# Three probability buffers, a wait moved behind the transposes, an earlier copy of the values, and the last head's blocks shared

## The reference

```
x = x + tanh(g0) * experts(layernorm(x))        # 4 experts, one per token by its id: (silu(h Wg) * (h Wu)) Wd
x = x + tanh(g1) * block(layernorm(x))

def block(r):                                   # 16 heads of 32, F = 2048, R = 16
    a = rmsnorm(r, ln1_w)
    scores = (a Wq.T)(a Wk.T).T / sqrt(32), causal; probs = softmax(scores)
    attn = (probs (a Wv.T)) Wo.T
    mod = 0.1 * tanh(attn @ A)
    h = rmsnorm(r, ln2_w)
    gate = silu(h W_in.T + mod * (h @ A) @ B)
    return r + (gate * (h W_up.T)) W_down.T
```

## Time and profile before

| | |
|---|---|
| median of three runs | 1045.88 us |
| profiled execution, its own time | 1046.06 us |
| its span, first to last instruction | 1044.3 us |
| PE, PEld busy | 1011.3 (97%), 831.4 (80%) us |
| DVE, ACT, POOL busy | 701.9 (67%), 608.0 (58%), 284.6 (27%) us |
| mean granted TensorE clock | 0.996 |
| attention phases | about 172 to 247, 392 to 468, 613 to 688, 833 to 909 us |

### The profile page before, as it was taken

How to read it: one execution, slowest core, us unless ns; L and a number is a source line. 1 busy time by engine, 2 the same in 40 slices (tenths; PEclk the granted TensorE clock), 3 DMA queues, 4 the chain that set the end, 5 groups by cost and what they waited for, 6 DMA issues and landing times.

```text
span 1044.3 us, 16780 instructions
## 1 busy us (share of the span) xinstructions
PE 1011.3 (97%) x5140; PEld 831.4 (80%) x5141; DVE 701.9 (67%) x1837; ACT 608.0 (58%) x1447; POOL 284.6 (27%) x280
## 2 busy tenths in 40 slices
PE   6999999999999999999999999999999989999998
PEld 6787888777888887778888888778888877788887
DVE  7766755996665558985665479966655599854443
ACT  4464456997344448985444369963444489844432
POOL 4536124861000117650000148610001177400000
PEclk9999999999999999999999999999999999999999
DMA  6545133343222426443322354432334253322221
GB/s 236 195 151 171 40 121 96 77 119 132 94 90 90 131 62 169 97 133 115 104 91 91 111 157 92 117 122 91 92 102 147 64 149 92 91 81 90 90 90 51
DMA packets 47073, 115.78 MB, mean 111 GB/s; under 512 B 6800, under 2 KB 6800, under 8 KB 46096
## 3 DMA queue, kind: packets, MB, share of 16 engines
q1 hardware_dynamic: 43968, 105.06, 33.7%
q0 software_dynamic: 3040, 9.96, 2.8%
HBM read 76.46 MB, written 13.37 MB: 86 GB/s over the span
## 4 chain that ended last, share of the span: by engine, by line
PE 86%; DVE 11%; issue 1%; DMA 1%; POOL 1%; ACT 1%; SPq 0%; DVEq 0%; POOLq 0%
PE bank L534 68%; PE bank L731 7%; DVE big L1399 5%; PE bank L793 4%; DVE wr L1385 3%; PE bank L697 2%; PE bank L835 1%; PE bank L590 1%; PE bank L764 1%; PE bank L605 1%; PE bank L648 1%; DMA stack<-wr 0%; PE bank L570 0%; POOL wr L502 0%; DVE big L1422 0%
## 5 line engine op out<-in xcount | busy, mean ns | idle before, releaser
L534 PE MATMUL bank<-hT,wr 128*128 128x512 f32 x1488 | 358.2, 390 | 0.0
L534 PEld LDWEIGHTS bank<-hT,wr 128*128 128x128 f32 x1488 | 279.2, 188 | 60.8 <-issue 1.5
L534 PE MATMUL bank<-wr,actr 128*128 128x512 f32 (+1 forms) x1224 | 303.4, 397 | 2.2 <-DVE actr L1367 1.5
L534 PEld LDWEIGHTS bank<-wr,actr 128*128 128x128 f32 x1224 | 228.9, 190 | 50.8 <-issue 3.0
L490 POOL TENSOR_SCALAR big<-big,rr 128x256 f32<-128x256 f32 (+1 forms) x128 | 154.5, 1215 | 82.4 <-DVE rr L1405 82.4
L429 POOL TENSOR_TENSOR wqs<-wstage,wqs 128x512 fp32r<-128x512 f32 x32 | 43.1, 1358 | 433.6 <-ACT wqs L949 432.2
L1432 DVE SCALAR_TENSOR_TENSOR wr<-stream,lns,wr 128x256 fp32r<-128x256 f32 x256 | 121.7, 537 | 52.2 <-ACT wr L1059 52.2
L1033 ACT ACTIVATE big<-big,nb 128x512 f32<-128x512 f32 (+3 forms) x256 | 140.9, 557 | 11.5 <-DVE nb L1399 11.1
L1385 DVE TENSOR_TENSOR wr<-bank,wr 128x512 fp32r<-128x512 f32 (+1 forms) x224 | 126.0, 607 | 21.3 <-ACT wr L949 20.7
L949 ACT ACTIVATE wr<-bank 128x512 fp32r<-128x512 f32 (+1 forms) x224 | 110.1, 529 | 35.7 <-PE bank L534 20.2
L949 ACT ACTIVATE actr<-act_sb 128x512 fp32r<-128x512 f32 x64 | 40.4, 632 | 146.0 <-DVE act_sb L1446 146.0
(11 more groups left out here) (174 smaller groups left out, 988.0 us busy)
## 6 DMA issues: line engine op xcount, KB each, us to landing
stream<-in_wmlp SPq DMA_DIRECT2D x64, 512.0 KB, 4.0
stack<-wr SPq DMA_DIRECT2D x192, 128.0 KB, 2.3
stream<-in_wmlp SPq DMA_DIRECT2D x64, 256.0 KB, 2.7
big<-in_x SPq DMA_DIRECT2D x4, 1024.0 KB
big<-y_rows SPq DMA_DIRECT2D x4, 1024.0 KB, 5.8
residual<-big SPq DMA_DIRECT2D x4, 1024.0 KB
big<-residual SPq DMA_DIRECT2D x4, 1024.0 KB, 6.5
out<-big SPq DMA_DIRECT2D x3, 1024.0 KB, 4.8
```

The source lines that it names most:

```text
L534: mm = pe.matmul(dst, lhs(pl, k), rhs(pr, k), start=start and i == 0, stop=stop and i == n - 1, skip_group_check=skip)
```

## The change

Five edits.

1. Three probability buffers instead of two, taken by head modulo 3; the third lies at column 2048 of `big`, in `hb`. The maxima of head n wait for the transposes of head n-3, and those of heads 0 to 2 for none. The load of y now also waits for all transposes of its batch.
2. PE's wait for the low part of the values moves from the head of the step to the first `attend`.
3. DVE's copy of the second values moves from step 0 to the end of the preamble, in front of the reciprocal of head 1.
4. In the last head of a batch DVE normalises the 512- and the 384-wide block, and GpSimd the 256-wide alone.
5. `exponentials` and `normalise` get the head instead of its parity.

```diff
+PACKED, NP = 1280, 3
+NORM_DVE, NORM_ACT, NORM_POOL = (3,), 0, (1, 2)
+LAST_DVE, LAST_POOL = (3, 2), (1,)
+POOL_ROWS = len(NORM_POOL) * (H - 1) + len(LAST_POOL)
...
-        prob = [flat[:, 4096 + PACKED * k:4096 + PACKED * (k + 1)] for k in range(2)]
+        prob = [flat[:, at:at + PACKED] for at in (4096, 4096 + PACKED, 2048)]
...
                 sp.wait_ge(hb_turned, b * TT)
+                sp.wait_ge(p_turned, b * (H * 3))
                 sp.dma_start(hb, rows).then_inc(y_in, 16)
...
-                for qt in NORM_POOL:
-                    rows = prob_rows(n % 2, qt)
+                for qt in NORM_POOL if n % H < H - 1 else LAST_POOL:
+                    rows = prob_rows(n % H, qt)
...
-                if j == 0:
-                    pe.wait_ge(vst_lo, b * NQ + q + 1)
                 if head < H - 1:
                     wait_probs(n + 1)
...
                 if head < H - 1:
                     first, second, third, last = (0, 1, 3, 2) if head == 0 else TURN_ORDER
+                    if j == 0:
+                        pe.wait_ge(vst_lo, b * NQ + q + 1)
                     attend(first, HI)
...
-                if not first:
-                    dve.wait_ge(p_turned, (n - 1) * 3)
+                if n % H >= NP:
+                    dve.wait_ge(p_turned, (n - NP + 1) * 3)
...
-                rows = prob_rows(par, NORM_DVE)
-                v.tensor_scalar(rows, rows, rr[:, par, NORM_DVE:NORM_DVE + 1], None, ALU.mult).then_inc(pn_ok, 1)
+                for qt in NORM_DVE if n % H < H - 1 else LAST_DVE:
+                    rows = prob_rows(n % H, qt)
+                    ins = v.tensor_scalar(rows, rows, rr[:, par, qt:qt + 1], None, ALU.mult)
+                ins.then_inc(pn_ok, 1)
...
-                if q == 0 and j == 0:
-                    dve.wait_ge(vp_done, b * 2 + 2)
-                    v.tensor_copy(vp[:, 2:4, :, :].rearrange("p t h r -> p (t h r)"),
-                                  bank[VALUES[1]][:, :]).then_inc(vpb_ok, 1)
...
                 qk_low(b, 1, 1, SECOND_K)
+                dve.wait_ge(vp_done, b * 2 + 2)
+                v.tensor_copy(vp[:, 2:4, :, :].rearrange("p t h r -> p (t h r)"),
+                              bank[VALUES[1]][:, :]).then_inc(vpb_ok, 1)
```

More of the change, by code:

```diff
@@ L43 @@
 TURNED = {0: (4, 0, 0), 1: (5, 0, 512), 3: (5, 384, 896), 2: (6, 0, 1024)}
-PACKED = 1280
-NORM_DVE, NORM_ACT, NORM_POOL = 3, 0, (1, 2)
+PACKED, NP = 1280, 3
+NORM_DVE, NORM_ACT, NORM_POOL = (3,), 0, (1, 2)
+LAST_DVE, LAST_POOL = (3, 2), (1,)
+POOL_ROWS = len(NORM_POOL) * (H - 1) + len(LAST_POOL)
 TURN_ORDER = (2, 1, 3, 0)
@@ L230, in build, with prob_rows @@
         d_done, fin_out, out_in = sem("d_done"), sem("fin_out"), sem("out_in")
-        def prob_rows(par, qt):
+        def prob_rows(head, qt):
             at = SCORE[qt][2]
-            return prob[par][:, at:at + P * (qt + 1)]
+            return prob[head % NP][:, at:at + P * (qt + 1)]
         def gu_view(cols):
@@ L731, in turn @@
                 mm = pe.transpose(bank[bk][:, col + (qt - kt) * P:col + (qt - kt) * P + P],
-                                  prob[par][:, src:src + P], ident[:, :])
+                                  prob[n % H % NP][:, src:src + P], ident[:, :])
                 if qt == TT - 1 and kt != 1:
@@ L745, in wait_probs @@
                 pe.wait_ge(pn_act, n + 1)
-                pe.wait_ge(pn_pool, (n + 1) * len(NORM_POOL))
+                last = n % H == H - 1
+                pe.wait_ge(pn_pool, n // H * POOL_ROWS + (POOL_ROWS if last else (n % H + 1) * len(NORM_POOL)))
             def stack_loads(b, head):
@@ L1026, in split_qk, with exponentials, normalise @@
                 copy(qk[:, q % 2, (Q_HI, K_HI)[which], :], bank[at][:, :]).then_inc(qk_hi, 1)
-            def exponentials(n, par):
+            def exponentials(n, head):
+                par = head % 2
                 for i, qt in enumerate((3, 2, 0, 1)):
                     act.wait_ge(nb_ok, n * 4 + i + 1)
-                    rows = prob_rows(par, qt)
+                    rows = prob_rows(head, qt)
                     a.activation(rows, rows, ACT.Exp, bias=nb[:, par, qt:qt + 1], scale=-1.0,
                                  accum_out=rs[:, par, qt:qt + 1]).then_inc(exp_ok, 1)
-            def normalise(n, par):
+            def normalise(n, head):
+                par = head % 2
                 act.wait_ge(rr_ok, n + 1)
-                rows = prob_rows(par, NORM_ACT)
+                rows = prob_rows(head, NORM_ACT)
                 a.activation(rows, rows, ACT.Copy, scale=rr[:, par, NORM_ACT:NORM_ACT + 1]).then_inc(pn_act, 1)
@@ L1043, in head_step @@
                 if q < NQ - 1 or j < QH - 1:
-                    exponentials(n + 1, (j + 1) % 2)
+                    exponentials(n + 1, q * QH + j + 1)
                 if (q, j) in COPY_AT:
@@ L1051, in head_step @@
                     if i == 0 and (q < NQ - 1 or j < QH - 1):
-                        normalise(n + 1, (j + 1) % 2)
+                        normalise(n + 1, q * QH + j + 1)
             def split_gate_up(b, c, par):
@@ L1389, in qk_low, with maxima @@
                 low(qk[:, q % 2, (Q_LO, K_LO)[which], :], bank[at][:, :], qk[:, q % 2, (Q_HI, K_HI)[which], :], qk_lo)
-            def maxima(n, par, first=False):
-                if not first:
-                    dve.wait_ge(p_turned, (n - 1) * 3)
+            def maxima(n, par):
+                if n % H >= NP:
+                    dve.wait_ge(p_turned, (n - NP + 1) * 3)
                 for i, qts in enumerate(((3,), (2, 0), (1,))):
@@ L1398, in maxima @@
                         bk, col, _ = SCORE[qt]
-                        v.tensor_tensor_reduce(prob_rows(par, qt), bank[bk][:, col:col + P * (qt + 1)],
+                        v.tensor_tensor_reduce(prob_rows(n % H, qt), bank[bk][:, col:col + P * (qt + 1)],
                                                masks[:, S - P * (qt + 1):S], -1.0, 3.0e38, ALU.add, ALU.min,
@@ L1521, in batch @@
                 dve.wait_ge(res_out, (b + 1) * 16)
-                maxima(b * H, 0, first=True)
+                maxima(b * H, 0)
                 gate_up_low(b, 1, 1)
@@ L1525, in batch @@
                 qk_low(b, 1, 0)
-                maxima(b * H + 1, 1, first=True)
+                maxima(b * H + 1, 1)
                 qk_low(b, 1, 1, SECOND_K)
+                dve.wait_ge(vp_done, b * 2 + 2)
+                v.tensor_copy(vp[:, 2:4, :, :].rearrange("p t h r -> p (t h r)"),
+                              bank[VALUES[1]][:, :]).then_inc(vpb_ok, 1)
                 for q in range(NQ):
```

## The result

The changed kernel took 1035.17 us (median of 5 runs, 1034.66 to 1039.15) against 1046.36 for the kernel before in the same comparison: a ratio of 0.9899 (95% interval 0.9883 to 0.9914), 1.0% faster. The forecast was 1038, with a range of 1034 to 1043. The profiled execution took 1034.66 us, with a span of 1032.9, which is 11.4 us less than the 1044.3 of before.

What follows compares the result with a forecast made beforehand. Chain of waits 86% PE, 11% DVE, so only what holds PE in attention counts. Per batch 1.1+0.6+0.1=1.8 us; 4x1.8+0.97=8.2 us, giving 1038 us, range 1034 to 1043.

Steps and rivals of the forecast that it cites:

- Turn 1: PE's ten transposes of head 1's probabilities: the 2.1 us values wait goes, transposes end 1.05 us sooner.
- Turn 2: PE's transposes of head 2: GpSimd's queue holds them, so their start gains 0.4 us, not 2.1.
- Heads 2 to 8: Six attention steps run at 25.5 us as in batch 1; with the earlier 0.4, 1.0 us gained at T(8), head 8's transposes.
- The late steps: DVE's reciprocals of heads 10 to 15: 0.12 us saved per step, bounds 0 and 0.22; 0.6 us a batch.
- The last head: End of each batch's attention: GpSimd normalising one block instead of two gains at most 0.1 us.
- The clock: Batch 1 behind its values wait: the lower-clock stretch goes, 1.53 us more there, +0.97 after a 0.56 us deduction.
- The load of y: 1 MB load delayed ahead of chunk 2's weights: 2.6 us plus 0.6 issue, 0.8 us to spare, cost 0.
- Rival D: Late y load holds chunk 2's weights on SP: 3x1.7=5.1 us given back, 1043; chance 5%.
- A: Attention: saturated ScalarE and DVE eat the third buffer's gain; only 4.2 us saved, 1042; chance 15%.
- B: Attention: GpSimd is ready when PE is, so the whole wait comes back; 13 us saved, 1033; chance 9%.
- C: Attention: DVE normalisations meet GpSimd work more often, 0.90 us each; 3.5 us slower, 1049.5; chance 8%.
- E: Lower clock level comes at other places, about 1.5 us each, moving the result inside the range; no chance given.

Runs made afterwards that it cites:

- the late copy: Changed kernel with DVE's copy of the second values put back behind the maxima of head 2: 1038.24 us, ratio 0.9907 to the kernel before.
- The start alone: Kernel before, two buffers and old last head, with only the wait for the values moved and the second values copied sooner: 1041.73 us, ratio 0.994.
- the wait of two: Changed kernel with three buffers, but the maxima wait for the transposes one head later, as with two buffers: 1041.56 us, ratio 0.9945.
- less work on DVE alone: Changed kernel with DVE normalising only 8 of 512 columns in heads 10 to 14, leaving out part of the computation: 1036.51 us, ratio 0.9895.
- the old last head: Changed kernel with the last head's blocks shared as before, DVE 512 wide, GpSimd 256 and 384: 1037.34 us, ratio 0.9904.
- everything but the start: Kernel before with three buffers and the late load of y; old wait for the values, old copy, old last head: 1041.95 us, ratio 0.995.
- the late y load: Kernel before with one added wait, so the load of y waits for the batch's transposes: 1047.76 us, ratio 1.0007.
- weights later: Changed kernel with GpSimd's preparation of the third key projection moved from head step 0 to 1, behind head 2's normalisation: 1036.4 us, ratio 0.9896.
- shared heads 1 and 2: Changed kernel with the last head's split between DVE and GpSimd used in heads 1 and 2 too: 1038.97 us, ratio 0.9918.
- the last comparison: Comparison in which the unaltered changed kernel was measured once more against the kernel before: 1035.54 us, ratio 0.9888.

## Why the forecast held, and which terms were off

**Turn 1, as forecast.** The wait for the values is gone, and T(1) falls from 5.03 to 3.59 us after turn 0. What turn 1 then waits for is GpSimd's normalisation, 0.63 us (I gave about 0.4), and the late copy would have cost 0.45 (I gave 0.6). I had turn 1 start the moment GpSimd ended; GpSimd's last block ends at 179.06+2.36=181.42 and PE starts at 181.66, 0.24 us later.

**Turn 2, as forecast.** GpSimd's queue holds it: a wait of 0.52 us, and a gain of 0.48 (I gave 0.4). T(2)-T(1) is 5.29, where 5.6 was forecast.

**Heads 2 to 8, right in size by luck, wrong in cause.** I gave 1.0 us at T(8) and it is 0.94 in batch 0 and 1.02 in batch 2. I put 0.6 of it down to three buffers. The start alone gives 35.45-34.44=1.01 with two, and three with the old start give 0.2 from T(2) to T(8). The meeting with GpSimd in head step 3 is weaker when DVE comes sooner: 1.04 us in batch 2 in place of 1.38.

**The late steps, mis-sized.** I gave 0.12 us a step between bounds of 0 and 0.22, and it is 0.22, the upper bound: 5x0.22=1.1 us, not 0.6. The kernel with the wait of two shows that this wait is the term. My reason for 0.12 was that ScalarE bounds next, with 0.12 us free. That ScalarE fills up is right (less work on DVE alone did not shorten the step); how much it had free was wrong. The window before shows it busy 15.65 of 16 us, 0.09 us idle a step, and still its step became 0.22 shorter: its operations overlap when they follow closely, and part of its idle time was a wait for DVE's maximum, which came sooner as well. The clause behind the colon is read from the order of the work and not tested by itself.

**The last head, mis-sized.** I gave at most 0.1 us, from GpSimd's 2.44 us beside PE's own work in the long steps. It is worth 0.25, in short steps and in long ones, as the variants with the old last head and with the wait of two show. What I had wrong is when PE was free. I took the end of the low rank products' row, 242.32 us, and saw 0.09 us of idle time. But PE can start a turn under the end of that row, 0.91 us after the products' start, as it does when only one block is left to GpSimd. In the kernel before it started after 1.16 us, 0.26 us after GpSimd's end at 242.15, so the second block did hold it.

**The clock, right.** Batch 1's stretch is gone, 1.53 us as worked out. In the three profiles with the wait of about 2 us for the values such a stretch followed it in one batch (the kernel before), one (everything but the start), and three of four (the late y load, at 403.9, 625.8 and 847.6 us). In the changed kernel's two profiles none followed turn 1. The 1.27 us of the earlier stretch, near 37 us, are in no term of my sum: the second profile of the changed kernel has that stretch as well.

**The load of y, right.** Here is the 512 KB part of chunk 2 that is needed first, issued at 241.94, then its first use (a DMA row is target, queue, KB, us to landing):

```profile
stream<-in_wmlp SPq DMA_DIRECT2D x1, 512.0 KB, 8.4
```

```profile
251.41 1.70 ACT L1065 ACTIVATE wr<-stream,lns 128x256 fp32r<-128x256 f32 x4
```

It takes 2.4 us longer from issue to landing than in the earlier trace rows and lands at 250.34, with 1.07 us to spare (forecast: 2.6 and 0.8). Rival D is refuted here and by the experiment with that load alone.

**The sum.** Undisturbed batch 2 gained 2.37 us: 1.00 for the start, 0.27 for the last head (0.25 with the old one put back) and the rest, 1.10, for the buffers. I gave 1.8, and the missing 0.6 is 0.5 for the late steps and 0.2 for the last head, less 0.1 that the start fell short. Four such batches are 9.5; batch 1 has 0.7 more (its clock, less a late load), batch 3 0.4 more (its turn 1 comes at 3.19), batch 0 0.5 less (a late load, below), which is 10.0 where I gave 8.2. The profile's other 1.27 us, at the early stretch, are not the change's.

**The rivals.** A (4.2 us, the full engines eat it) is refuted by the late steps; B (13 us) because GpSimd still holds turn 2, and when it was made to come sooner (weights later) the gain was lost by turn 8. C did not come as a loss, but its mechanism is real. The changed kernel has seven 512 wide normalisations longer than 0.6 us where before had three, as C said; each is shorter (batch 2: 0.72 and 1.04 us where before had one of 1.38), and in all they take 2.9 us more than 0.49 us each, against 2.8 before. The same meetings ate the gain of the weights one step later and turned the shared heads 1 and 2 into losses. E, the clock at other places, came too (last section), and stayed inside the range: 1034.66 to 1039.15 us.

The forecast weighed a rule from the Trainium skill, "SBUF — State Buffer", section "Who interferes with whom": one of the two engines holds the ports for its whole instruction. The page says it of DVE instructions in a mode that uses both pairs of ports, which a tensor_scalar can be in; no trace here shows the mode. At the last head the trace does not bear the rule out. GpSimd, then DVE in time, last head of batch 3:

```profile
890.03 1.23 POOL L493 TENSOR_SCALAR big<-big,rr 128x256 f32<-128x256 f32 x1 [1.35 <-DVE rr L1411]
```

```profile
889.97 0.49 DVE L1415 TENSOR_SCALAR big<-big,rr 128x512 f32<-128x512 f32 x1
890.37 0.64 DVE L1415 TENSOR_SCALAR big<-big,rr 128x384 f32<-128x384 f32 x1
890.93 1.60 DVE L1391 TENSOR_TENSOR wr<-bank,wr 128x256 fp32r<-128x256 f32 x3
```

DVE's second block ends at 891.01 and GpSimd's work only at 891.26: the block took 0.64 us and was not held to the end, though it took longer than the wider one in front of it (0.49). The low parts began 0.96 us after the first block did, so about 0.56 later than without the block, between my 0.4 and the 1.05 by the rule. Against GpSimd's work on the weights the rule does hold: DVE ended 0.21 to 0.29 us after a subtraction in every meeting shown, and 0.29 us after a one-input cast in this one (head 2 of batch 0 in the changed kernel):

```profile
182.52 0.61 POOL L428 CAST wqs<-wstage 128x512 fp32r<-128x512 f32 x1
```

```profile
182.70 0.72 DVE L1415 TENSOR_SCALAR big<-big,rr 128x512 f32<-128x512 f32 x1
```

What sets these GpSimd operations apart from its normalisations is open.

## What to carry to other kernels

Measure the starts of a repeated step from the first of its phase, for every phase, in both profiles: that ledger separates what a change did from clock stretches and from gains of earlier phases, and its differences (0.25 us) are far below what the total can tell. When a wait on a full engine goes, take the idle time of that engine as the gain until a second engine is shown to be full without being held by the first, and test that by relieving each engine alone. Do not take the end of a row of matmuls for the moment when the next can start; look at how soon behind their start it comes when nothing holds it. Before an engine's work is moved forward, look at what the other engine is doing in that moment: here each meeting of a DVE normalisation with a GpSimd subtraction cost 0.4 to 1.0 us, up to as much as the move was worth.

## What was not expected of the hardware

**A small load that lands late.** One late step, turn 10 to 11, took 4.62 and 4.44 us in batches 0 and 1 of the changed kernel, and 3.93 in batches 2 and 3. The chain of waits, batch 0 (start, us, what):

```profile
218.47 0.56 SPq L321
...
219.08 0.61 SPq L321
...
219.72 3.93 DMA stack<-wr
...
223.70 0.50 PE bank L700
```

The load of a stack of q or k, issued as always, landed after 3.93 us; it usually takes 2.3. The same happened in kernels with two buffers, so the change is not its cause. What delays it stays open. The steps behind it are shorter, and at turn 15 0.51 and 0.30 us are left of it (61.22 and 61.01 us against 60.71 in batch 2). It can be worse. PE waiting for such a load, in the changed kernel's second profile (landed after 6.24 us) and in the profile with less work on DVE (6.72 us), batch 3 of each:

```profile
842.70 0.50 PE L700 MATMUL bank<-stack 96*128 96x512 f32 x1 [1.20 <-DMA stack<-wr]
```

```profile
841.15 0.50 PE L700 MATMUL bank<-stack 96*128 96x512 f32 x1 [2.05 <-DMA stack<-wr]
```

**The clock between executions.** The changed kernel ran at a mean granted clock of 1.0 in 1034.66 us and at 0.997 in 1039.0 and 1039.15: 4 us between executions of one kernel. The clock is not all of it: in the last comparison an execution at 1.0 took 1036.81. The row of before at 36 us shows what a stretch is: 0.72 over 6 us is (1-0.72)x6/0.5=3.4 us at the lower level (1.2 GHz). In the same profile the wait of 2.1 us was followed by one in one batch and not in three. Of the ten kernels with the shortened wait, eight reached a mean clock of 1.0 in some execution, and the kernel before in none of 39; but one of the ten, with less work on DVE, had a stretch at 841.6 us in batch 3 all the same. It followed the wait of 2.05 us shown above. In the attention phases of the 14 kept profiles PE waited 1.5 to 2.1 us thirteen times, twelve for the values and once for this load, and each of the six stretches there came right behind one of these waits (of 2.0 to 2.1 us). Which of the waits are followed by one is not settled by these runs.
